# Message stage of a graph network kernel: the last two output components opened by a bf16 product of zeros, and a third product buffer

## The reference

```python
x = x + _L1_gnn_ref(_layernorm(x), node_vec1, src, dst, edge_attr_4, edge_attr_8, ...)

# in _L1_gnn_ref, MUL = 64:
w_a, w_b, w_c, w_d = ...                       # 4 x 64 weights for each edge
xg0, xg1 = y0[edge_src], y1[edge_src]          # 64 scalars, 64 vectors of the source node
mid0 = w_a * xg0 * ea0
mid1 = w_b * einsum('euc,ec->eu', xg1, ea1) * INV_SQRT3
mid2 = (w_c * xg0)[:, :, None] * ea1[:, None, :]
mid3 = (w_d * ea0)[:, :, None] * xg1
agg = segment_sum(concatenate([mid0, mid1, mid2, mid3]), edge_dst, num_segments=n)
```

## Time and profile before

| | us |
|---|---|
| median of 3 runs | 2367.6 (2365.4 to 2368.01) |
| the profiled execution | 2366.55 |
| its span | 2364.5 |

### The profile page before, as it was taken

One profiled execution on the slowest core, in us unless ns is written; L12 is line 12 of the kernel. 1 busy time (PEld: TensorE's weight loads), 2 busy tenths in 40 slices (PEclk: granted clock), 3 DMA queues, 4 the chain that ended last, 5 costly groups with the idle time before them and its releaser, 6 DMA issues. The chain is left out here.

```text
span 2364.5 us, 37045 instructions
## 1 busy us (share of the span) xinstructions
PE 1939.7 (82%) x10646; PEld 1596.8 (68%) x10646; DVE 1135.9 (48%) x2491; ACT 1031.6 (44%) x3208; POOL 1152.2 (49%) x1143
## 2 busy tenths in 40 slices
PE   2788888888688767999466988888888878959998
PEld 1555555555356647999345978878778875649997
DVE  5433333333322664444557877777777742141111
ACT  3444444444034402332265766666666626513332
POOL 1777777777600005555107777777777700002221
PEclk7899999999689558999677999999999998959999
DMA  9667676676300118999716766666666604036663
GB/s 237 182 219 223 211 224 222 212 223 211 107 18 0 55 39 293 352 353 343 194 44 198 205 185 194 190 190 189 188 189 190 176 21 92 22 107 200 199 200 98
DMA packets 273478, 413.50 MB, mean 175 GB/s; under 512 B 67662, under 2 KB 162500, under 8 KB 273053
## 3 DMA queue, kind: packets, MB, share of 16 engines
q1 hardware_dynamic: 218056, 258.46, 35.7%
q0 software_dynamic: 54784, 150.16, 21.4%
q10 hardware_dynamic: 462, 2.76, 0.4%
HBM read 324.41 MB, written 87.84 MB: 174 GB/s over the span
## 5 line engine op out<-in xcount | busy, mean ns | idle before, releaser
L1725 POOL DMA_INDIRECT msg_got<-y_dram,pair_src x464 | 505.5, 1090 | 241.8 <-issue 132.5
L1738 ACT ACTIVATE msg_scaled<-msg_plain,msg_w 128x125 f32<-128x125 f32 x1392 | 415.9, 386 | 234.5 <-DVE msg_plain L1774 224.2
L632 POOL DMA_INDIRECT sum_got<-xn_dram,pair_src x464 | 438.9, 946 | 156.1 <-issue 131.6
L673 PEld LDWEIGHTS sum_ps_sum<-sum_got,sum_onehot 128*125 128x125 f32 x928 | 178.9, 200 | 239.7 <-issue 198.7
L673 PE MATMUL sum_ps_sum<-sum_got,sum_onehot 128*125 128x256 f32 x928 | 262.3, 408 | 92.4 <-DMA sum_got<-xn_dram,pair_src 91.9
L1248 ACT ACTIVATE ffn_run_hid<-ffn_run_ps_h,cols 128x128 f32<-128x128 f32 x512 | 145.9, 368 | 391.0 <-PE ffn_run_ps_h L1207 391.0
L1756 PE MATMUL msg_ps_z<-msg_prod,msg_plain 128*125 128x256 f32 x928 | 244.4, 386 | 83.7 <-ACT msg_scaled L1738 41.0
L1765 PEld LDWEIGHTS msg_ps_z<-msg_prod,msg_scaled 128*125 128x125 f32 x2320 | 290.0, 188 | 13.2
L1765 PE MATMUL msg_ps_z<-msg_prod,msg_scaled 128*125 128x128 f32 x2320 | 291.4, 273 | 0.0
L732 DVE TENSOR_TENSOR agg<-sum_ps_sum,agg 125x256 f32 x232 | 98.5, 425 | 373.4 <-PE sum_ps_sum L673 373.4
L703 ACT ACTIVATE sum_wide<-sum_ps_w,sum_rec 128x128 f32<-128x128 f32 x416 | 130.0, 364 | 285.5 <-PE sum_ps_w L659 285.5
(11 more groups left out here) (294 smaller groups left out, 2409.8 us busy)
## 6 DMA issues: line engine op xcount, KB each, us to landing
ffn_run_w<-in_L_ffn_w SPq DMA_DIRECT2D x128, 512.0 KB, 6.6
msg_w<-edge_w SPq DMA_DIRECT2D x232, 260.0 KB
edge_w<-sum_wide SPq DMA_DIRECT2D x52, 1040.0 KB, 4.9
ffn_run_w<-in_L_ffn_Wd SPq DMA_DIRECT2D x32, 1024.0 KB, 5.6
sum_got<-xn_dram,pair_src POOLq DMA_INDIRECT x464, 3.0
msg_got<-y_dram,pair_src POOLq DMA_INDIRECT x464
ffn_rows<-xn SPq DMA_DIRECT2D x10, 560.0 KB
table_got<-ffn_results SPq DMA_DIRECT2D x10, 560.0 KB
```

What stands on the lines that cost most here:

```text
L632: pool.indirect_dma_start(got[:, n % RING, u, :], None, k.xn_dram, bass.IndirectOffsetOnAxis(ap=k.pair_src[:, n, u:u + 1].bitcast(U32), ax ...
L673: last = pe.matmul(ps_sum[n % ZB][0:P, :], onehot[n % OB][:, u, :], got[:, n % RING, u, :], start=(u == 0), stop=(u == KC - 1))
L1725: pool.indirect_dma_start(got[:, s % RS, c, :, :].rearrange("p k v -> p (k v)"), None, k.y_dram, bass.IndirectOffsetOnAxis(ap=k.pair_src[: ...
L1738: last = act.activation(scaled[s % MB][:, x, c, :], plain[s % MB][:, c, :], ACT.Copy, scale=w[:, s % RS, c, D + x:D + x + 1])
```

## The change

The buffers `prod` shrink from 12 planes to 8 and become three. The zero planes are gone; in their place a row `zeros` of 128 bf16 zeros is made once. For each pair, behind the first L1756 product, PE multiplies it by a row of ones (bf16, one row deep, 128 columns) into planes 6 and 7 of the result. The first scaled product is then 128 columns wide like the others. `products(s)` waits for PE's step s-3.

```diff
@@ -1686,7 +1686,7 @@
 def sum_messages(nc, k):
 
 
-    RS, MB, ZB = 4, 3, 6
+    RS, MB, ZB, XB = 4, 3, 6, 3
     CH = 2 * KC
     NST = NPAIR // 2
     assert NST * 2 == NPAIR
@@ -1695,12 +1695,13 @@
         got = ph.sb("got", [128, RS, CH, 4, MUL])
         plain = [ph.sb(f"plain{b}", [128, CH, P]) for b in range(MB)]
         scaled = [ph.sb(f"scaled{b}", [128, 3, CH, P]) for b in range(MB)]
-        prod = [ph.sb(f"prod{b}", [128, CH, 12, MUL]) for b in range(2)]
+        prod = [ph.sb(f"prod{b}", [128, CH, 8, MUL]) for b in range(XB)]
         ps_z = [ph.ps(f"z{b}", [128, 8, MUL]) for b in range(ZB)]
+        zeros, zeros_made = ph.sb("zeros", [1, 2 * MUL], BF16), ph.sem("zeros_made")
         ps_lanes, lanes_made = ph.ps("lanes", [128, P]), ph.sem("lanes_made")
         w_in, got_in = ph.sems("w_in", RS), ph.sems("got_in", RS)
-        masked, scaled_made, made, summed, added, zeroed = (
-            ph.sem(x) for x in ("masked", "scaled_made", "made", "summed", "added", "zeroed"))
+        masked, scaled_made, made, summed, added = (
+            ph.sem(x) for x in ("masked", "scaled_made", "made", "summed", "added"))
         block = ph.ctx.enter_context(nc.Block())
 
         @block.sync
@@ -1742,28 +1743,25 @@
         @block.tensor
         def _(pe):
             pe.matmul(ps_lanes[:, :], k.onesf[0:1, :], k.iota[0:1, 0:P], start=True, stop=True).then_inc(lanes_made, 1)
-            pe.wait_ge(zeroed, 2)
+            pe.wait_ge(zeros_made, 1)
             for s in range(NST):
                 pe.wait_ge(scaled_made, s + 1)
                 pe.wait_ge(made, s + 1)
                 if s >= ZB // 2:
                     pe.wait_ge(added, 1 + 2 * (s - ZB // 2 + 1))
-                mask, by, p = plain[s % MB], scaled[s % MB], prod[s % 2]
+                mask, by, p = plain[s % MB], scaled[s % MB], prod[s % XB]
                 for h in range(2):
                     z = ps_z[(2 * s + h) % ZB]
                     for u in range(KC):
                         c = KC * h + u
                         pe.matmul(z[0:P, 0:4, :], mask[:, c, :], p[:, c, 0:4, :], start=(u == 0), stop=False)
+                        if u == 0:
+                            pe.matmul(z[0:P, 6:8, :].rearrange("p k v -> p (k v)"), k.ones[0:1, 0:P], zeros[0:1, :], start=False, stop=False)
                     for x in range(3):
                         for u in range(KC):
                             c = KC * h + u
-                            if x == 0 and u == 0:
-                                last = pe.matmul(z[0:P, 4:8, :].rearrange("p (o k) v -> p o k v", o=2), by[:, x, c, :],
-                                                 p[:, c, 4:12, :].rearrange("p (o k) v -> p o k v", o=2)[:, :, 0:4:3, :],
-                                                 start=False, stop=False)
-                            else:
-                                last = pe.matmul(z[0:P, 4:6 + x:1 + x, :], by[:, x, c, :], p[:, c, 4 + x:8:3 - x, :],
-                                                 start=False, stop=(x == 2 and u == KC - 1))
+                            last = pe.matmul(z[0:P, 4:6 + x:1 + x, :], by[:, x, c, :], p[:, c, 4 + x:8:3 - x, :],
+                                             start=False, stop=(x == 2 and u == KC - 1))
                 last.then_inc(summed, 1)
 
         @block.vector
@@ -1776,12 +1774,12 @@
                                   .to_broadcast([128, CH, P]), ALU.is_equal).then_inc(masked, 1)
 
             def products(s):
-                p = prod[s % 2]
+                p = prod[s % XB]
                 y, v = got[:, s % RS, :, :, :], w[:, s % RS, :, 0:D].rearrange("p c (k v) -> p c k v", v=MUL)
                 dve.wait_ge(w_in[s % RS], 32 * (s // RS + 1))
                 dve.wait_ge(got_in[s % RS], 64 * (s // RS + 1))
-                if s >= 2:
-                    dve.wait_ge(summed, s - 1)
+                if s >= XB:
+                    dve.wait_ge(summed, s - XB + 1)
                 dve.tensor_tensor(p[:, :, 0:8:7, :], v[:, :, 0:4:3, :], y[:, :, 0:1, :].to_broadcast([128, CH, 2, MUL]), ALU.mult)
                 dve.tensor_tensor(p[:, :, 1:4, :], v[:, :, 1:2, :].to_broadcast([128, CH, 3, MUL]), y[:, :, 1:4, :], ALU.mult)
                 dve.tensor_tensor(p[:, :, 4:7, :], v[:, :, 2:3, :].to_broadcast([128, CH, 3, MUL]), y[:, :, 1:4, :], ALU.mult)\
@@ -1798,8 +1796,7 @@
 
             dve.wait_ge(lanes_made, 1)
             mask(0)
-            for b in range(2):
-                dve.memset(prod[b][:, :, 8:12, :], 0.0).then_inc(zeroed, 1)
+            dve.memset(zeros[:, :], 0.0).then_inc(zeros_made, 1)
             dve.memset(k.agg[:, :, :], 0.0).then_inc(added, 1)
             for s in range(NST):
                 if s + 1 < NST:
```

## The result

| | median us | lowest to highest | runs |
|---|---|---|---|
| before | 2366.91 | 2362.19 to 2373.2 | 14 |
| after | 2373.14 | 2367.27 to 2381.19 | 14 |

The ratio is 1.0029, with an interval of 1.0016 to 1.0042: the changed kernel is slower by 0.29%, and the medians stand 6.2 us apart. The forecast was no change: 2367.4 us, in a range from 2362 to 2373. The profiled execution of the changed kernel took 2367.27 us, the lowest of its fourteen (span 2365.5 us). So the difference is not to be read from the two spans, but from the stage of the messages in both traces.

A forecast was written before the change was run, and what follows sets the result against it. POOL's gathers were taken to bound the message stage. Terms of 0 + 0 + 0 - 0.2 us on the profiled 2366.55 gave 2366.3, and with the run median 1.05 above the profiled run 2367.4 us, range 2362 to 2373.

The forecast's parts named there:

- POOL is the bound: Message stage: POOL's gathers never wait for a buffer, only fixed 0.3 us gaps, 5.58 us a step against PE's 4.78.
- The zero planes: PE's pairs in the message stage: one fp32 product shrinks from 256 to 128 columns, 0.42 us a step less.
- The bf16 product: PE's added product of zeros in each pair: 0.10 us taken, bounds 0.055 and 0.28, making PE's step 4.56 us.
- Third buffer, memsets: DVE's weaker wait for PE and its shorter clearing at the stage's start: both 0 on POOL's path.
- The tail: PE's one step after the last gather is on the path: -0.22 us, ends -0.31 and +0.14.
- What DVE does to POOL: Two DVE products a pair cost the gathers 67 us; landings set when they meet, so PE's change adds 0.
- D: Rival: DVE's products meet the gathers more dearly, at the 1117 ns pattern, 2380 us; chance 0.04.
- C: Rival: faster PE lets DVE's products meet the gathers more cheaply, at the 1068 ns pattern, 2357 us; chance 0.05.
- B: Rival: PE paces the message stage after all, so 26 us would go, 2342 us; chance 0.04.
- E: Rival: PE, less busy, drops to the 1.2 GHz clock for part of the time, 2425 us at half; chance 0.02.

The follow-up runs named there:

- two_buffers: The changed kernel with two product buffers in place of three; 2373.08 us, ratio 1.0038 to the kernel before.
- bf16_full: The changed kernel with the bf16 product of zeros over all 128 rows in place of one; 2368.93 us, ratio 1.0017 to the kernel before.
- spread kernels: The changed kernel and the kernel before, each with the memset of `agg` in five parts behind the products of steps 0 to 4; 2370.57 and 2366.60 us.
- paced_after: The changed kernel with one more bf16 product of zeros, over all 128 rows, in each step's first pair; 2337.94 us, ratio 0.9890.
- fp32_row: The changed kernel with the product of zeros in fp32 instead of bf16, still one row deep; 2373.54 us, ratio 1.0040.
- early_again: Repeat: changed kernel, first 18 steps with full-row products of zeros, two a pair; 2606.69 us where the kernel before took 2610.26.

## Why the prediction was wrong

**POOL is the bound.** Right: gaps of 0.3 us only, in both traces.

**The zero planes, -0.42 us a step.** Right: the six scaled products of a pair take 1.31 us in after (1302.53 to 1303.84), twelve records of 0.109 us, where they took 1.52 before (1504.31 to 1505.83). That is 0.21 us a pair.

**The bf16 product.** A term mis-sized: "I take 0.10 us, nearer to the low end". It measures 0.39 us, beyond my upper bound of 0.28. That bound added a load and a matmul end to end; it left out that its neighbours lose their overlap too, 0.10 us on either side. So PE's step rose by 0.36 us and didn't fall by 0.22. The price stands for all rows only.

**Third buffer, memsets: nothing.** Right for the buffer (two_buffers). For the memsets I looked at POOL's gaps alone, and they show nothing; but the earlier products meet other gathers, at 1.47 us in steps 3 and 4 for 1.04, a cost of 0.4 us.

**The tail.** The right place, the wrong sign: from the same mis-sized term, +0.36 for -0.22 us; measured +0.5 us behind the last gather.

**What DVE does to POOL.** The step that failed: "How much each costs depends on when it meets a gather, and that is set by landings, which PE does not touch", and with it "the phase is redrawn by each landing". It doesn't hold in the first fifteen steps. My own reading had the row for it: DVE waits for PE 15 times, "in the first steps". There the meeting is set by PE's period, and it repeats: 0.80 us of hindrance in two steps became 1.50. Of the 4.7 us by which the gathers grew in the two traces, 4.3 lie in steps 5 to 15, behind the 0.4 of the memsets. From step 16 on the traces show 601 and 602 ns. That the two are so nearly equal is partly luck, for other traces spread over 33 ns, and the spread kernels show a loss of 1.4 to 5.5 us that isn't in the first steps. Had I had 0.10 us right, this step would have failed all the same (bf16_full: 1.0017 [1.0003 to 1.0032]).

**The rivals.** D (dearer meeting) was right in kind and sign; I had it decide from 10 ns of the mean gather, and it came with exactly that, 1100 against 1090. Its price of +12.5 us for a whole stage was too high, for it showed in only 13 steps. Its 0.04 was too low, since the reason against it was the step that failed. C had the same mechanism with the other sign; paced_after shows that it exists. B is out: it needed PE's step above the gathers', and 5.13 us is still below their 5.62. E is out: clock 1.00. With the terms as measured the sum is 2366.9 + 4.7 + 0.5 = 2372.1 us; the measured median is 2373.1, and the interval of the ratio is a rise of 3.8 to 9.9 us.

**Shown and argued.** Shown: the price of a product by its rows; the cycles in nine traces; that a held cheap cycle gives 1%. Read from traces and not isolated by a run: that most of the loss of after lies in steps 3 to 15, and that the period and not the start of the products picks the cycle. Not shown: which whole number a given period falls into, and where the rest of the loss lies.

## What to carry to other kernels

A saturated engine isn't safe from the others: when a second engine hinders it at a fixed period, the cost is that period less a whole number of the saturated engine's own, so shortening an engine that is "off the path" can cost time and lengthening it can gain (here 1.1%). Which whole number comes about has to be tried: here 5.24 and 5.27 us fell into the cheap cycle, 5.13 and 5.16 did not. Look for the stretches where a hindering engine waits for a third one, however short they are: there the third sets the meeting. And a small product between large ones should use all 128 rows: here that cost 0.10 us, and one or 64 rows cost 0.39.

## What was not expected of the hardware

A product on one row between full ones isn't overlapped with either neighbour, and one on 64 rows costs the same 0.39 us. In paced_after both kinds stand in one stream of weight loads:

```profile
1854.45 0.13 PEld L1759 LDWEIGHTS msg_ps_z<-msg_zeros,ones 1*125 1x125 bf16 x1 [0.33 <-issue]
...
1854.97 0.14 PEld L1761 LDWEIGHTS msg_ps_z<-msg_zeros,ones 128*125 128x125 bf16 x1
```

Their matmuls start at 1854.45 and 1855.18 us: the full-row load goes 0.21 us ahead of its matmul, the one-row load starts with it, and so does the load of the L1757 behind it (the list from after above, 1301.99). The Trainium skill, page "TensorE: Matmul & The Clock Gate", section "Step-by-step: what each phase is for", has weight loads pulled ahead of matmuls in flight; here that holds between full-row products, and on neither side of the one-row one.

A gather of 0.946 us takes up to 1.75 us beside DVE products in after, and 2.93 us once in fp32_row; in the kernel before this costs some 67 us of 647. The time of a gather chain isn't one number: the same kernel takes 2364 to 2367 us on some chips and 2610 to 2623 on others. Both layers with gathers are longer there. The first layer's gathers end at 734 us in early_again and at 643 in before, and the message stage takes 800 us for 658, while the stages behind it take 460 us in both.
